# One-pass tail for the expert stage, later splits in the row stages, and 68 instead of 84 pair adds in the edge stage

## The reference

```python
x = x + L0_gnn(layernorm(x), src, dst, edge_attr_20, edge_weight, edge_attr_4)   # messages per edge, summed by src
x = x + L0_ffn(layernorm(x))      # one of 64 experts a row: h = x Wd, a spline by table, y = hs Wu
x = x + L1_gnn(layernorm(x), edge_index, node_vec1)                             # 4 blocks, below
x = x + L1_ffn(layernorm(x))      # gated, weights rounded to -1, 0, 1 times a group's mean

# L1_gnn, 4 times:
y = cond_layer_norm(x, cond, s1, b1)
ex = exp(q[src] . k[dst] - max);  attn = ex / sum over a src     # one term for each edge, duplicates too
x = x + (sum of attn * v[dst]) @ wo + bo
y = cond_layer_norm(x, cond, s2, b2)
x = x + relu(y @ m_w1 + m_b1) @ m_w2 + m_b2

# L0_ffn, the last step: y = einsum(hs, Wu[tidx]) * scale[tidx];  x = x + y
```

## Time and profile before

| | |
|---|---|
| median of 3 runs | 3019.26 us (3016.41 to 3020.27) |
| the profiled execution | 3022.77 us, of which the traced span is 3021.0 us |
| mean granted TensorE clock | 0.927 |
| busy: PE, DVE, ACT, POOL | 2551.6, 1880.1, 1365.9, 1187.2 us |
| edges | about 72 to 573.5 us |
| experts | about 706 to 1031 us |
| plain norm | 1031 to 1045.4 us |
| first rows stage | 1045.4 to 1178.6 us |
| attention blocks, with their row stages | 1178.6 to 2721 us |
| last rows and feed-forward | 2721 to 3021 us |

### The profile page before, as it was taken

The page is one execution under the profiler, slowest core; times in us unless marked ns, Lnnn a source line. Parts: engine busy times, 40 slices in busy tenths (PEclk is TensorE's granted clock), DMA queues, the critical chain, the costliest instruction groups (busy, mean ns, idle before and its releaser), DMA issues. The chain is left out here.

```text
span 3021.0 us, 38863 instructions
## 1 busy us (share of the span) xinstructions
PE 2551.6 (84%) x13585; PEld 2188.0 (72%) x13585; DVE 1880.1 (62%) x3536; ACT 1365.9 (45%) x2725; POOL 1187.2 (39%) x918
## 2 busy tenths in 40 slices
PE   3999999735867078997998998989989989988999
PEld 3787777534646067896786886878868878876997
DVE  2888888562563345676745776546767467766862
ACT  1555565421244143664434664435644356644431
POOL 2888888784632201225102224012242022362420
PEclk9999999767878579999999999999999999999999
DMA  7434344217639711101112101211011121121101
GB/s 244 91 77 80 71 81 78 23 9 225 187 96 292 207 38 51 34 17 52 60 40 61 42 27 42 82 52 34 18 52 59 41 62 40 33 68 42 53 22 34
DMA packets 172004, 220.42 MB, mean 73 GB/s; under 512 B 111710, under 2 KB 120345, under 8 KB 164384
## 3 DMA queue, kind: packets, MB, share of 16 engines
q1 hardware_dynamic: 80253, 170.59, 19.4%
q0 software_dynamic: 91552, 47.27, 7.8%
HBM read 177.10 MB, written 40.15 MB: 72 GB/s over the span
## 5 line engine op out<-in xcount | busy, mean ns | idle before, releaser
L2104 POOL TENSOR_SCALAR prob<-prob,rden,linked 125x1250 f32<-125x1250 f32 x160 | 223.5, 1397 | 923.7 <-DVE rden L2071 923.7
L579 POOL DMA_INDIRECT pairs<-late_cnt,late_idx x160 | 361.8, 2261 | 109.7 <-DMA pairs<-late_cnt,late_idx 55.9
L2022 ACT CAST prob_high<-ps 125x375 fp32r<-125x375 f32 (+1 forms) x480 | 230.9, 503 | 266.8 <-PE ps L1984 266.4
L2063 DVE CUSTOM_DVE_ANT_0 prob<-ps,mask 125x1250 f32<-125x1250 f32 x160 | 233.1, 1457 | 127.7 <-PE ps L1960 109.2
L2076 DVE TENSOR_TENSOR prob_low<-ps,prob_high 125x375 fp32r<-125x375 f32 (+1 forms) x480 | 270.0, 585 | 46.6 <-ACT prob_high L2022 46.5
L538 PE MATMUL ps<-onehot,mhi 125*128 125x512 f32 (+1 forms) x960 | 254.8, 375 | 19.0 <-DVE onehot L426 18.9
L1973 PE MATMUL ps<-ident,prob 125*125 125x125 f32 x1600 | 252.4, 273 | 17.3 <-POOL prob L2104 10.7
L338 POOL DMA_INDIRECT Hg<-h_rows,dsti x160 | 223.4, 1396 | 103.3 <-issue 98.2
L1973 PEld LDWEIGHTS ps<-ident,prob 125*125 125x125 f32 x1600 | 232.3, 187 | 29.7 <-POOL prob L2104 22.9
L538 PE MATMUL ps<-onehot,mlo 125*128 125x512 f32 (+1 forms) x960 | 244.5, 364 | 0.0
L2014 ACT ACTIVATE prob<-prob,top 125x1250 f32<-125x1250 f32 x160 | 214.7, 1342 | 44.4 <-DVE top L2063 35.4
(11 more groups left out here) (408 smaller groups left out, 6110.4 us busy)
## 6 DMA issues: line engine op xcount, KB each, us to landing
mask<-mask_d SPq DMA_DIRECT2D x40, 546.9 KB
sg_wd<-L_ffn_Wd SPq DMA_DIRECT2D x32, 512.0 KB, 6.8
w_ring<-L_ffn_Wd SPq DMA_DIRECT2D x16, 1024.0 KB
w_ring<-L_ffn_Wu SPq DMA_DIRECT2D x16, 1024.0 KB
pairs<-zeros POOLq DMA_DIRECT2D x18, 625.0 KB, 25.5
keyrow<-keys_d SPq DMA_DIRECT2D x40, 244.1 KB
kept<-g_d SPq DMA_DIRECT2D x40, 224.0 KB
g_d<-kept SPq DMA_DIRECT2D x30, 224.0 KB
```

Source lines behind the costliest of these rows:

```text
L579: nc.gpsimd.indirect_dma_start(pairs[a][:, :], bass.IndirectOffsetOnAxis(T.E.late_idx[:, c:c + 1], 0), T.E.late_cnt[:, c:c + 1], None, com ...
L2022: s.copy(M.pt[0][:, n % 3, 0:w], T.ps[0:P, 3 + n % 4, 0:w]).then_inc(high, 1)
L2063: v.tensor_tensor_reduce(M.prob[:, r, :], S(u)[0:P, 0:N], M.mask[:, it % MASKS, :], 1.0, 3.0e38, ALU.add, ALU.min, M.top[:, r:r + 1]).then ...
L2104: nc.gpsimd.tensor_scalar(M.prob[:, r, :], M.prob[:, r, :], M.rden[:, r:r + 1], T.linked[:, it:it + 1], ALU.mult, ALU.mult).then_inc(norme ...
```

## The change

Five edits; `mask_d`, `x_d` and `g_d` are the same memory as before, and the computed values are the same.

1. 68 of the pair adds stand in the edge stage, 60 of them spread over the groups and the rest in the last two; the expert stage opens with 58 instead of 42.
2. The expert stage's end is one pass. POOL gathers the result without waiting for mask tile 8 (SP stores the last two mask tiles); DVE adds each row as it lands and norms it at once, ACT writes the normed row; SP spills rows and normed rows, and loads the condition's weights and `wq` of the first rows stage, all inside this stage. `plain_norm` is gone. An eighth logarithm stands in the up phase.
3. In the "attn" row stages the four splits stand at tiles 4 to 7 instead of 2 to 5, the carries begin at tile 8 instead of 6.
4. In the last stage the second unit of the first weight group stands ahead of the turning of the second group's weights; DVE's low half of row tile 9 stands ahead of the measuring of these weights.
5. Buffers are placed earlier (`Map` takes a base), so that the normed rows can be written while the expert stage runs.

```diff
-EARLY_ADDS = 84
+EARLY_ADDS = 68
+PACED_ADDS = 60
@@ edges, POOL
-                        more = EARLY_ADDS * (g + 1) // NG
+                        more = PACED_ADDS * (g + 1) // NG if g < NG - 2 else EARLY_ADDS - 4 * (NG - 1 - g)
@@ experts
-LN0, LNSTEP, LNS = 12, 8, 7
+LN0, LNSTEP, LNS = 12, 8, 8
@@ experts, SP
+                    for p in range(0, CR, 32):
+                        sp.dma_start(T.cw[p:p + CH + 1, :, :]..., A["L1_gnn_cond1"][0:1]...).then_inc(rows_in, 16)
                     for g in range(RG, 2 * NGRP):
                         load(g)
                     for t in range(NS_T):
                         sp.wait_ge(yc_act, t + 1)
                         sp.dma_start(y_d[...], ysb[:, t, :]).then_inc(y_stored, 16)
+                    for t in range(NT - 2, NT):
+                        sp.wait_ge(l_ready, t + 1)
+                        wide(sp, mask_d[t * P:(t + 1) * P, :], pl[t % 2], mask_last)
+                    sp.dma_start(place.raw_b[:]..., A["L1_gnn_wq"][0:1]...).then_inc(rows_in, 16)
+                    sp.wait_ge(added, NT)
+                    wide(sp, x_d..., T.X, T.spilled)
+                    sp.wait_ge(rows_made, NT)
+                    wide(sp, g_d..., first, T.spilled)
@@ experts, POOL
                         if t >= 1:
-                            pool.wait_ge(l_ready, t)
                             if t == NT - 1:
                                 gather()
+                                break
+                            pool.wait_ge(l_ready, t)
                             wide(g, mask_d[(t - 1) * P:t * P, :], pl[(t - 1) % 2], pst[(t - 1) % 2])
@@ experts, DVE (ACT has Sqrt and Identity to match)
-                    for t in range(NT):
-                        dve.wait_ge(g_in[t], 16)
-                        v.scalar_tensor_tensor(T.X[:, t, :], yg[:, t, :], R.scale[:, t:t + 1], T.X[:, t, :],
-                                               ALU.mult, ALU.add).then_inc(added, 1)
+                    for t in range(NT + 1):
+                        if t < NT:
+                            ... the same addition
+                            v.bn_stats(...); v.bn_aggr(...)
+                        if t >= 1:
+                            dve.wait_ge(row_std, t)
+                            v.reciprocal(...)
+                            v.scalar_tensor_tensor(T.shift[:, t - 1:t], T.mv[:, t - 1, 0:1], -1.0, T.rstd[:, t - 1:t], ...)
@@ rows_stage, POOL
-                        if 2 <= t < KD + 2:
-                            split(t - 2)
-                        if t >= 6:
-                            carry(t - 6)
-                    for t in range(NT - 6, NT):
+                        if 4 <= t < KD + 4:
+                            split(t - 4)
+                        if t >= 8:
+                            carry(t - 8)
+                    for t in range(NT - 8, NT):
                         carry(t)
@@ last stage, PE
                     unit(NS * j)
                     if j == 0:
                         turn_y(NT - 1)
+                        unit(1)
                     if j + 1 < KF:
                         turn_w(j + 1)
-                    unit(NS * j + 1)
+                    if j > 0:
+                        unit(NS * j + 1)
@@ last stage, DVE
                 low_y(NT - 2)
+                low_y(NT - 1)
                 measure(1)
-                low_y(NT - 1)
                 choose(1)
```

More of the change, by code:

```diff
@@ L973, in group_loaded, with experts @@
     return n
-def experts(nc, T, A, R, xs_d, y_d, pairs, mask_d):
+def experts(nc, T, A, R, xs_d, y_d, pairs, mask_d, x_d, g_d, place):
     with ExitStack() as ctx:
@@ L985, in experts @@
         yT, ysb = xsT, xs
-        yg = ring[:].rearrange("p g s d -> p (g s) d")[0:P, 0:NT, :]
+        yg = ring[:].rearrange("p g s d -> p (g s) d")[0:P, RG * WG - NT:RG * WG, :]
+        first = place.first
         tables = A["L0_ffn_splines"].rearrange("e k g h -> e (k g h)")
@@ L1279, in _ @@
                         logarithm(t)
+                    for t in range(NT + 1):
+                        if t < NT:
+                            act.wait_ge(row_step, 2 * t + 2)
+                            s.activation(T.std[:, t:t + 1], T.mv[:, t, 1:2], ACT.Sqrt, bias=T.eps[0:P, :]).then_inc(row_std, 1)
+                        if t >= 1:
+                            act.wait_ge(row_scale, 2 * t)
+                            s.activation(first[:, t - 1, :], T.X[:, t - 1, :], ACT.Identity, bias=T.shift[:, t - 1:t],
+                                         scale=T.rstd[:, t - 1:t]).then_inc(rows_made, 1)
                 @block.vector
@@ L1411, in expert_layer @@
             route(nc, T, A, xf, sc, xs_d, R, pairs)
-        experts(nc, T, A, R, xs_d, y_d, pairs, mask_d)
+        experts(nc, T, A, R, xs_d, y_d, pairs, mask_d, x_d, g_d, place)
 H, DH = 4, 128
@@ L1559, in _ @@
                     load(1)
-                loads(sp, cw_in, b_in, w_in, bias_in)
+                loads(sp, b_in, w_in, bias_in)
                 if source == "attn":
@@ L2125, in qkv_loads, with loads @@
         def qkv_loads(L, first):
-            def loads(sp, cw_in, b_in, w_in, bias_in):
-                if first:
-                    load_cond(sp, L, 1, cw_in)
-                sp.dma_start(flat(M.raw_b), one(par("wq", L))).then_inc(w_in, 16)
+            def loads(sp, b_in, w_in, bias_in):
+                if not first:
+                    sp.dma_start(flat(M.raw_b), one(par("wq", L))).then_inc(w_in, 16)
                 sp.dma_start(bqk[:, 0, :], one(par("bq", L))).then_inc(b_in, 16)
```

97 lines of the change are left out of this document (50 added, 47 removed).

## The result

The changed kernel takes 2949.64 us (median of 4 runs, 2945.10 to 2950.85) against 3017.84 for the one before (4 runs), a ratio of 0.9773, 95% interval 0.9756 to 0.9790: 68 us less, and 63 to 74 by the interval. The forecast was 2917, with 2895 to 2945 by its own bounds and 2888 to 2965 with the rivals.

The account below looks back on a forecast made before the run. PE, busy 84% of the span, was taken as the bound, so only its waits pay: -29 - 32 + 2 - 44 + 1 = -102 from 3022.8 gives 2920.8, median 2917; range 2895 to 2945, with rivals 2888 to 2965.

Parts of the forecast that it names:

- edges: Edge stage: fewer POOL adds between gathers let PE set the pace; -29 us (range -34 to -18).
- experts and tail, with SP's loads: Expert stage: one-pass end brings cwr earlier despite a later up phase, -32 us; extra SP loads +2.
- attn row stages: Attn row stages: moving splits breaks the circle of waits, 12 us a stage less 1 for holds; -44 us.
- last stage, from its rows on: Last stage: an extra unit fills PE's weight wait but measuring starts 6 us later; +1 us (-4 to +4).
- The 13 adds behind the last gathers: Edge stage's end: POOL runs 13 adds until 541.4 us, then drains to 544.5, giving back 3 us.
- the pace stays (D): Edges: rows' landing, not POOL's issue, is late, so gathered-row waits stay; 2946 us, chance 0.08.
- The sixteen adds: Expert stage: adds moved in delay count loads into busy transfers; up phase ends 8.5 us later (+4 to +15).
- The tail: Experts' end: gathers wait only for y_d stored, cwr 32 us earlier, up phase's 8.5 included (-20 to -38).
- SP issues three loads more, 0.90 us: Experts: three loads ahead of the down phase's weights, with PE close behind; +2 us (0 to 3).
- the two spills cost nothing: Experts' end: 5 MB of stores of x and normed rows precede the rows stage's later weights; 0, 3 at worst.
- Rival A: Attn row stages: DVE's shift waits for POOL's runs, so the stages give only 14 us; 2947 us, chance 0.13.
- rival B: Edges and experts: late adds and count loads leave gains of 15 in edges, 2 in tail; 2961 us, chance 0.12.

Follow-up runs that it names:

- only_edges: Kernel before with edit 1 alone (60 paced adds, 68 in all, in the edges): 3009.92 us, ratio 0.9971.
- adds72: Changed kernel with condition loads behind expert weights, X spilled in pieces, last stage's old order, and 72 edge adds instead of 68: 2925.29 us, ratio 0.9692.
- less16: Changed kernel with condition loads behind expert weights, X spilled in pieces, last stage's old order, and the last 16 pair adds omitted: 2918.09 us, ratio 0.9683.
- cond_late: Changed kernel with the three loads of the condition's weights moved behind all expert weight loads in SP's program: 2947.66 us, ratio 0.9761.
- cond16: Changed kernel with each 17-row load of the condition's weights cut into 16 rows and one, at the same place: 2937.95 us, ratio 0.9743.
- x_pieces: Changed kernel with X spilled in five pieces of two tiles, each once its rows are added, instead of one: 2939.71 us, ratio 0.9742.
- ffn_old: Changed kernel with the last stage's order as before (all of edit 4 undone): 2936.81 us, ratio 0.9734.
- only_split: Kernel before with only the attn row stages' splits moved to tiles 4 to 7, carries left from tile 6: 2970.82 us, ratio 0.9838.

## Why the prediction was right or wrong

By the profiled executions, from the forecast's own sum (-102) to what the trace has (-77.6):

| step | forecast | trace |
|---|---|---|
| edges | -29 | -26 |
| experts and tail, with SP's loads | -30 | -6 |
| attn row stages | -44 | -56 |
| last stage, from its rows on | +1 | +7 |
| the rest (attention, other stages) | 0 | +3 |

The experts' term is the one that failed: the time there hardly fell. The last stage's lies outside its bounds too (-4 to +4), and the -56 of this pair is beyond the -52 that I had allowed; by medians it is 45 (below).

**Edges: right.** PE sets the pace (busy for 414 of the 420 us from 100 to 520), 11.4 us a group against 11.24 assumed; the last add and PE's last matmul end together, at 544.5 and 545.3, where I had 541.4 and 541.6. The 13 adds behind the last gathers did return 2 to 3 us. The rival that the pace stays (D) is out: the waits for rows are gone. One execution alone would not give the 26 us: over the nine with 68 adds PE's last matmul ends at 547.2 in the mean, over the three with 84 at 572.8.

**The sixteen adds: direction right, size 8.5 against 10.9 alone.** The forecast said that the loads of the first two tiles leave a time without transfers and go into a full one. only_edges shows that, and also what I had only as a bound: the first logarithm stops ACT's copies, and PE behind them, for 15 us. adds72 and less16 show the cost as a step between +180 and +191; my later theory, a fixed 100 us behind the first load, put only_edges too late and doesn't fit ffn_mid. In the changed kernel itself this cost is hidden behind a larger one (next paragraph). With 9 us in all, the edge part alone is worth a third of what it gives its own stage.

**The tail: right that it shortens, wrong by 24 us in size.** Of its four terms, each came out worse. (1) The up phase's end: +8.5 and +2 forecast, +15.8 measured. In the changed kernel's trace 14.4 of these lie ahead of the up phase. The term "SP issues three loads more, 0.90 us" was the wrong question: the issue is short, but the transfer stood 12.8 us in front of weights. The loads and the adds hide each other: the adds alone make the copies 10.9 us late (only_edges), both together 15.8. So taking away only the loads gave nothing (cond_late, cond16), and only with four adds back as well (adds72) did the copies come 12 us earlier. What the loads cost without the adds no run shows. (2) The gathers' start: I took 8 us behind the copies for the stores of `y_d`; it is 13.9, as long as the wait that was removed (13.1). So "the gathers wait for no mask tile" gave nothing by itself; a second condition was due at nearly the same time. Nothing in rows 6 or 7 shows when those stores land, and I should have bounded this from above by the 13.1. (3) From the first gather to the last normed row 32.6 us instead of 28: the first landing took 12.7 us from its issue, where I had 6.5. (4) From there to `cwr` 10.8 instead of 2.5: SP's hold. I had written that the two spills cost nothing, 3 at worst, and had asked only whether later weights come in time, not what SP's own issue does before a barrier. In the kernel before, the two spills stand 12 us apart, with the norm between them. x_pieces shows the size, 8 us. That a full queue is what holds SP is the likely reading; what the runs show is that the hold goes when `X` has left in pieces.

**Row stages: right.** Alone the edit gives 45 us by medians, 44 forecast. The 56 of the profiled pair have some 6 more in the first stage than in the others, where the kernel before had the hold of 7.52 us. I took that hold for a rare one. The second execution profiled with the old order (only_edges) has it at the same place:

```profile
1421.76 7.50 DVE L1820 SCALAR_TENSOR_TENSOR shift<-mv,rstd 125x1 f32<-125x1 f32 x1
```

Of the eleven profiled with edit 3 none has one above 1.3 us, so it may belong to the old order; two executions don't settle it. The split's tiles take 4.4 us, 4.2 forecast. Rival A (the lock eats it) is out: in the changed kernel `shift` takes 0.85 to 0.89 us in three tiles of each "attn" stage and never over 1.0, and no long hold came. POOL's run of eight carries, which I feared up to 10 us for, held nothing.

**Last stage: right in its steps, off in size.** I had one unit filling one wait and the measuring 6 us late, and called it +1. It is +4 to +5 in this pair, since the unit needs the same row as the measuring: PE waits 1.47 us for it, and 5.24 stay. (The other 2 of the table's 7 lie ahead of the first turning; what they are stays open.)

**The range held, in part by luck.** The forecast's own bounds, 2895 to 2945, did not hold: 2949.64 lies above them, mainly because the experts and their tail gave 6 us and not the 17 that were the least by my bounds (-20, and +3 for the loads). The wide range held because rival B, the edges' gain taken back in the experts, had been priced. It stood at 44 us for edges and experts; 27 came, 3 in the edges and 24 in the experts. But in the changed kernel they came by other ways than B's late count loads: by the loads of the condition's weights, the stores of the result, the first landing and SP's hold.

## What to carry to other kernels

Where a wait for several things is taken away in part, look up when the others come: the last but one is often nearly as late, and bounds the gain from above. An engine that only issues transfers is part of a barrier; ask before each stage's end what its queue holds. And when work moves from one stage to a later one, look whether it pushes a transfer out of a quiet time into a full one: here that cost was nearly a step, and once the loads of the condition's weights were out of the way, taking back four of the sixteen adds took back the whole of it. Two delays that end at the same place hide each other: removing one shows nothing until the other is gone too.

## What the runs showed of the hardware

- Three transfers of 17 partitions each (68 KB in rows of 4 KB, with the condition's weights) went row after row: their 51 packets took 12.8 us in the changed kernel, beside the weights. In a later stage of the kernel before they took 8.2 us (1451.4 to 1459.6), with the DMA engines at a mean share of 0.10. Each cut into 16 rows and one, all 51 were done in about 2 us. Weights issued 1 us behind the uncut ones landed 16 us after their issue, while the core's transfers ran at 370 GB/s.
- SP's issue of a 260 KB transfer of 13 partitions took 9.07 us right behind 2.5 MB of the same kind (9.06 and 9.08 in cond_late and ffn_old, 4.21 in cond16), and 0.31 us when that had gone out in five pieces.
- DVE's small `shift` with three POOL operations beside it in each tile takes 0.63 to 0.89 us instead of 0.16. Longer holds are few: 7.52 and 7.50 us in the two executions profiled with the old order, up to 2.45 us in only_split, and 1.3 us at most in the eleven with edit 3.
